# State-space stage of a two-layer block: the product of step size and input moves from GpSimd to VectorE

## The reference, cut to what matters

```python
x = silu(conv(x))                                        # (B, L, E)
delta = softplus((x @ wd1.T) @ wd2.T + wd2_b)            # step size
def step(h, inp):
    xt, dt, bt, ct = inp
    h = exp(dt[:, :, None] * A) * h + (dt * xt)[:, :, None] * bt[:, None, :]
    y = einsum('ben,bn->be', h, ct)
```

## Time and profile before

| | us |
|---|---|
| median of 3 runs | 2730.8 (2727.92 to 2732.36) |
| the profiled execution | 2736.76 |
| its span, first to last instruction | 2735.0 |
| state-space stage, first scan to last product | 858.8 to 1910.6 |

### The profile page before, as it was taken

The page is one execution under the profiler, slowest core; times in us unless marked ns, Lnnn a source line. Parts: engine busy times, 40 slices in busy tenths (PEclk is TensorE's granted clock), DMA queues, the critical chain, the costliest instruction groups (busy, mean ns, idle before and its releaser), DMA issues. The chain is left out here.

```text
span 2735.0 us, 34598 instructions
## 1 busy us (share of the span) xinstructions
PE 2182.1 (80%) x10642; PEld 1553.8 (57%) x10642; DVE 1949.4 (71%) x2745; ACT 1375.5 (50%) x2317; POOL 1152.8 (42%) x717
## 2 busy tenths in 40 slices
PE   2799999999746777877787878766699999999950
PEld 1677877777612233333333333222699999999950
DVE  6555545665413988979797978889588888888844
ACT  1332322333136656566566656633576666667620
POOL 1111221221127897979797979784000000000036
PEclk7899999999866989999899999989899999999975
DMA  6011001111011212222222222221555555555545
GB/s 241 16 39 38 32 6 38 38 38 38 27 50 48 101 61 102 80 98 73 89 81 82 83 81 73 82 82 57 212 223 223 223 223 215 212 212 211 208 161 166
DMA packets 115029, 298.50 MB, mean 109 GB/s; under 512 B 16820, under 2 KB 89540, under 8 KB 96148
## 3 DMA queue, kind: packets, MB, share of 16 engines
q1 hardware_dynamic: 108820, 280.97, 28.2%
q0 software_dynamic: 6144, 16.79, 1.9%
HBM read 247.45 MB, written 50.27 MB: 109 GB/s over the span
## 5 line engine op out<-in xcount | busy, mean ns | idle before, releaser
L1003 POOL TENSOR_TENSOR m_work<-m_ux,m_bb 128x1024 f32<-128x1024 f32 x256 | 598.1, 2354 | 55.5 <-DMA m_bb<-scratch_bT 33.6
L1144 ACT ACTIVATE m_da<-m_dl,m_A 128x512 f32<-128x512 f32 x512 | 349.5, 686 | 348.6 <-DVE m_hh L1201 343.9
L1285 PE MATMUL m_y<-m_work,m_ident 128*128 128x512 f32 x1024 | 504.6, 616 | 1.5 <-DVE m_work L1207 1.5
L1207 DVE TENSOR_TENSOR m_work<-m_hh,m_cb 128x1024 f32<-128x1024 f32 x256 | 312.6, 1221 | 106.3 <-PE m_cb L1266 84.3
L1770 POOL DMA_INDIRECT c_ya<-scratch_yg,c_dst x64 | 68.1, 1065 | 732.4 <-DMA c_wts<-scratch_wts 713.2
L1701 PE MATMUL e_h<-e_xTh,e_w1h 128*128 128x256 f32 x1248 | 356.0, 285 | 16.9 <-DVE e_xTl L1637 16.9
L1201 DVE TENSOR_TENSOR_SCAN m_hh<-m_da,m_work 128x512 f32<-128x512 f32 x256 | 298.3, 1207 | 93.5 <-POOL m_work L1003 92.3
L1701 PE MATMUL e_h<-e_xTh,e_w1l 128*128 128x256 f32 x1248 | 351.7, 282 | 0.0
L1701 PE MATMUL e_h<-e_xTl,e_w1h 128*128 128x256 f32 x1248 | 351.6, 282 | 0.0
L1201 DVE TENSOR_TENSOR_SCAN m_hh<-m_da,m_carry,m_work 128x512 f32<-128x512 f32 x256 | 313.7, 1267 | 1.6 <-POOL m_work L1003 1.5
L1285 PEld LDWEIGHTS m_y<-m_work,m_ident 128*128 128x128 f32 x1024 | 203.0, 198 | 176.9 <-issue 162.6
(11 more groups left out here) (249 smaller groups left out, 4713.7 us busy)
## 6 DMA issues: line engine op xcount, KB each, us to landing
e_w<-in_w SPq DMA_DIRECT2D x39, 2048.0 KB, 7.5
m_bb<-scratch_bT SPq DMA_DIRECT2D x64, 1024.0 KB, 4.8
e_w<-in_w SPq DMA_DIRECT2D x39, 1024.0 KB, 9.5
e_xg<-scratch_xg SPq DMA_DIRECT2D x39, 256.0 KB, 9.6
scratch_yg<-e_yo SPq DMA_DIRECT2D x39, 256.0 KB, 9.6
scratch_xg<-x1p SPq DMA_DIRECT2D x19, 512.0 KB, 7.8
e_b<-in_b SPq DMA_DIRECT2D x39, 128.0 KB, 8.6
xt<-in_x SPq DMA_DIRECT2D x9, 512.0 KB, 5.6
```

Of the source, the lines that this page charges most:

```text
L1003: pool.tensor_tensor(bx[:, u % NB], ux[q % 2][:, cols], slot.to_broadcast([P, HALF, T]), ALU.mult).then_inc(s_bx, 1)
L1144: act.activation(da[d % NA][:], dl[q % 2][:, e], ACT.Exp, scale=A[:, at:at + 1]).then_inc(s_exp, 1)
L1207: dve.tensor_tensor(hc[:, u % 4], hh[:, u % 2], cb[:].rearrange("p (o t) -> p o t", o=1).to_broadcast([P, HALF, T]), ALU.mult).then_inc(s_ ...
L1285: last = mm(y[:, i], ident[:], hc[:, u % 4, i], start=False, stop=(n % NST == NST - 1))
```

## The change

POOL no longer multiplies at n = 27. VectorE does, with the same waits and the same signal, once before its loop (for chunk 0) and then behind its product of half step 27 in chunks 0 to 6, for the chunk that follows.

```diff
@@ gpsimd, extra(q, n)
-                if n == 27:
-                    pool.wait_ge(s_dl, p + 1)
-                    pool.wait_ge(s_silu, 2 * p + 1)
-                    pool.tensor_tensor(ux[p % 2][:], dl[p % 2][:], xs[p % 2][:], ALU.mult).then_inc(s_ux, 1)
@@ vector
+            def times_x(p):
+                dve.wait_ge(s_dl, p + 1)
+                dve.wait_ge(s_silu, 2 * p + 1)
+                dve.tensor_tensor(ux[p % 2][:], dl[p % 2][:], xs[p % 2][:], ALU.mult).then_inc(s_ux, 1)
+
+            times_x(0)
             for u in range(STEPS):
@@ the end of the loop over u
                 if n == NST:
                     finish(q, 0)
+                if n == 27 and q + 1 < NCH:
+                    times_x(q + 1)
```

## The result

| | before | changed |
|---|---|---|
| median, us | 2731.3 (2727.9 to 2732.4, 4 runs) | 2779.3 (2773.9 to 2786.6, 4 runs) |
| the profiled execution, us | 2736.8 | 2786.6 |
| first to last product of the stage (their starts) | 861.23 to 1909.38 | 858.85 to 1959.79 |

The changed kernel is slower: ratio 1.018, 95% interval 1.015 to 1.021, so about +48 us, where +46.5 (2777) was forecast. All of it is in the loop of the state-space stage: from the first to the last product with `C` the loop took 1048.2 us, and now takes 1100.9, 52.8 more; its first product comes 2.4 us earlier.

The account below looks back on a forecast made before the run. VectorE's chain was taken as the bound, with TensorE's waits on top. Wait 21.8, product 16.0, hold 16.4, waits given back -14.6, start -2.1 and clock 9 gave +46.5 us, a median of 2777, range 2752 to 2791.

Parts of the forecast that it names:

- the hold: In the loop, VectorE's product is held by one GpSimd operation starting beside it, 2.35 us each, seven times: +16.4 us.
- the waits for `m_cb`: At half step 28 on, TensorE's clock falls after idle time and VectorE waits longer for its sums: 6 x 1.5 = +9 us.
- wait for `dl`, seven times: Behind half step 27 in chunks 0 to 6, VectorE stands still until GpSimd's L986 ends: 21.8 us.
- the product's own time, 7 x 2.29: Seven products lie in VectorE's chain in the loop at 2.29 us each: +16.0 us.
- waits for POOL given back: In the loop, VectorE's waits for GpSimd all go because GpSimd's queue is 4.5 us shorter a chunk: -14.6 us.
- start: At the stage's start VectorE's product replaces GpSimd's slower one ahead of the first scan: -2.1 us.
- The second sign in the prediction: The product's mean in the changed profile: 2.3 if nothing is held, 4.3 to 4.6 if one operation is.
- a sign of being wrong: Waits for m_cb falling because the pause lets ACT and PE catch up; they were forecast to rise by some 9.
- my faster rival: GpSimd's relief reaches ACT by the convolution sums, dl lands before half step 27: -18 us, 2713; chance 0.05.
- Nothing held: In the loop, the product runs beside GpSimd undisturbed: +30 us, 2761, or 2752 with no clock term; chance 0.24.
- Two operations in front: Two GpSimd operations precede the product, or the clock costs its full bound: 2790 to 2794; chance 0.07 together.

Follow-up runs that it names:

- e3: The changed kernel with VectorE's product behind half step 29 instead of 27; 2731.3 us, ratio 1.0001 to the kernel before.
- e1: The changed kernel, but GpSimd waits for s_ux right behind L986 and runs nothing beside VectorE's product; 2745.7 us, ratio 1.0057 to the kernel before.
- e2: The changed kernel, but GpSimd waits for s_ux behind the inputs of half step 30, so one operation stands beside the product; 2761.9 us, ratio 1.0119 to before.
- e4: The changed kernel with VectorE's product behind half step 30 instead of 27; 2744.0 us, ratio 1.0049 to the kernel before.
- e7b: The kernel before without the product: inputs read the step size, the factor xs is left out; 2715.3 us, ratio 0.9946 to the kernel before.
- e11: The changed kernel with four added GpSimd operations of 128x512 behind L986, then a wait for s_ux before the inputs of half step 30; 2774.7 us, one run.

## Why the prediction was right

The total was right within 2 us of 46.5, and that is luck: not every term was right, and two large errors, 14.5 too little for the hold and 15.1 too much for the waits for `m_cb`, cancelled. With the hold at its measured 30.9 and the rest as forecast the sum is +61.0, 2792, just outside the range. The direction, and that the new wait, the product and a hold are what the change costs, were no luck.

| term of the sum | forecast | changed kernel |
|---|---|---|
| wait for `dl`, seven times | +21.8 | +21.9 |
| the product's own time, 7 x 2.29 | +16.0 | +16.0 |
| held by POOL | +16.4 | +30.9 (7 x 4.42) |
| waits for POOL given back | -14.6 | -12.5 |
| start | -2.1 | -2.4 |
| waits for `m_cb` (TensorE's clock) | +9 | -6.1 |
| waits for `m_y` in `finish` | none | +5.0 |

The terms of the loop add up to +55.2, against the measured 52.8; the 2.4 between I can't assign. (The waits for `m_cb` are counted from the loop's first product on, 84.3 to 78.2.)

**The wait.** The step held in every chunk: POOL's way from ACT's L1129 to L986 was not touched, and the seven waits are 4.87, 1.56, 1.85, 1.50, 1.85, 1.73 and 8.49. The order of two events in the trace, the end of what DVE will wait for and the moment when DVE gets there, gave this term to 0.1 us. e3 shows that it was a matter of place alone.

**The hold.** That there would be one was right. The Trainium skill's rule in "SBUF — State Buffer", "Who interferes with whom", that a VectorE instruction with two SBUF inputs and a GpSimd instruction that reads SBUF exclude each other, agrees with e1 and e2: 2.29 against 4.42. So the engines do not meet at semaphores alone, as is said at the top: here one holds the other with no semaphore between them. The size was the step that failed: "I take one operation, 2.35 us". It was POOL's whole run up to its next stop, two operations, the other end of my bounds. The row I went by (L446, held by L298) had a single POOL operation beside it, and so could not tell one operation from all of them. The second sign in the prediction said so at once: the mean of the eight products is (2.29 + 7 x 6.71) / 8 = 6.16, not 4.35.

**The waits for `m_cb`.** The clock fell as forecast, and the waits at half step 30, where I had placed the cost, did rise: 1.24, 0.92, 0.20 and 1.01 in chunks 0, 2, 3 and 5, 3.4 together, against 0.83 before. I had taken 9. The sums did run at the low level, wholly or in part (3.05 to 3.62 in chunks 0 to 5, 1.88 at the high one), but the piece behind them only in part: it took 2.85, 1.98, 2.52, 2.05, 1.98 and 2.86 there, and DVE waited over 0.2 only where it took more than 2.5. What I had not seen is a gain elsewhere. All in all these waits fell, 84.3 to 78.2, which the prediction had named as a sign of being wrong. By half step:

| half step | before | changed kernel |
|---|---|---|
| 2 | 7.7 | 1.6 |
| 12 | 20.8 | 12.4 |
| 16 to 21 | 2.6 | 8.0 |
| 30 | 0.8 | 3.4 |
| 22, 24, 26 | 52.3 | 52.8 |

At half step 12 DVE waits for `m_cb` behind a piece that needs ACT's silu (L1064 before), and that needs POOL's last convolution sum. Before and changed, in chunk 3, DVE and the piece:

```profile
1306.77 1.22 DVE L1207 TENSOR_TENSOR m_work<-m_hh,m_cb 128x1024 f32<-128x1024 f32 x1 [4.05 <-PE m_cb L1266]
1301.14 5.37 PE L1237 MATMUL m_rb<-m_xs,m_w_x 128*96 128x512 f32 x8 [2.49 <-ACT m_mo L1097]
```

```profile
1328.47 1.22 DVE L1209 TENSOR_TENSOR m_work<-m_hh,m_cb 128x1024 f32<-128x1024 f32 x1 [1.81 <-PE m_cb L1270]
1324.55 3.67 PE L1241 MATMUL m_rb<-m_xs,m_w_x 128*96 128x512 f32 x8 [1.70 <-ACT m_mo L1093]
```

Before, ACT stood idle 0.80 us for POOL's sum ahead of the silu:

```profile
1294.25 1.91 ACT L1064 ACTIVATE m_xs<-m_spare 128x2048 f32<-128x2048 f32 x1 [0.80 <-POOL m_spare L946]
```

PE was then idle 2.49 us instead of 1.70, as much longer, and ran the piece at a granted clock of 0.68 instead of 1.00, in 5.37 us instead of 3.67. So most of what is saved here is TensorE's clock again, given back this time. Before, the piece took 5.22 to 5.37 in chunks 3 to 6; in the changed kernel it takes 3.67 wherever DVE waits for it. That is 6.6 of the 8.4 us. ACT's wait for the convolution sum, 5.2 before, is now:

```profile
ACT m_xs L1060 <- POOL m_spare L946: 1.6, 1, 1.6
```

In e4, where POOL was late again, it is 5.6, the piece takes 5.37 in four chunks, and the waits at half step 12 are 20.8 together, as before; in e7b and e1, where POOL is early, they are 12.4 each. So the road of my faster rival, from POOL's relief over the convolution sums to the pieces, exists. It is worth some 8 us, and the forecast had put it at nothing.

The waits at half step 2 are the clock as well: before, in chunks 0, 1, 2 and 6, the sums that open a chunk (L1283) took 3.2 to 3.8 us, where they take 1.9 to 2.0 at the high level, and in the changed kernel only chunk 2 has such a wait. In which chunks this happens changes from kernel to kernel, and why, the runs do not show; nor what lengthens the waits at half steps 16 to 21.

**The rivals.** Nothing held: refuted by e1 and e2. Two operations in front: right as a mechanism, but priced at 2790 to 2794 (2777 and 12 are 2789), since I added it to a clock term that did not come. Faster: its condition, `dl` ahead of half step 27, was met nowhere. Only its road from POOL's relief to the pieces was there. And e7b shows that even with no product on DVE the relief is worth 15 (10 to 20), less than the 16 to 18 that the product costs there.

## What to carry to other kernels

Before moving work to the engine whose chain sets the time, read from the trace when its input is ready and where the engine will be by then; and look at what the neighbour runs in that moment. A faster engine for an operation is no gain where the slow one had slack: here 36 us of GpSimd were worth 15, and VectorE needed 16. Ask rather which part of the operation is needed late: cutting it in two and leaving it on GpSimd gained 12, some 3.5 of them by VectorE's doing it at the start, where it idled. And a term that comes out right in total is not yet understood: here a hold twice as long was hidden by waits that got shorter elsewhere.

## What the runs showed of the hardware that was not expected

- A VectorE operation whose operands are all in SBUF, begun behind a running GpSimd operation, waited in the loops of this stage for all that GpSimd had ready, not only for the one in progress: 2.29, 4.42, 6.71 and 9.00 us with 0, 1, 2 and 3 operations. A memset of 0.10 us between two of them changed nothing (6.75, one run). It is no law: at the start of e11 the product was let in behind the first of four (3.11), and in the first stage L406 was through in 1.13 us in the middle of a row of eight.
- An operation with one tensor input can be held in the same way: 1.23 alone, 5.64 with two neighbours (one run).
- Scans and products with one operand in PSUM are not touched by any of this: 1.22 us for the product in every trace here, beside a busy GpSimd.
- A delay of 0.8 us on another engine can come back nearly threefold by way of TensorE's clock: behind 2.49 us of idle time instead of 1.70 a piece of eight matmuls took 5.37 us instead of 3.67 (granted clock 0.68 and 1.00), and VectorE waited 4.05 instead of 1.81.
